# A graph attention kernel on one core: the group loop written out instead of branched

## What is computed

```
alpha = (x @ wq) @ (x @ wk)^T;  alpha = relu(alpha) * (adj != 0);  softmax over axis 1
y     = layernorm(x + alpha @ (x @ weight))
q, k, v = y @ Wq + bq, y @ Wk + bk, y @ Wv + bv      (16 heads of 32)
s     = q k^T / sqrt(32), -inf where adj == 0;  softmax
out   = layernorm(y + (softmax(s) @ v) @ Wo + bo)
```

## Time and profile before

| | |
|---|---|
| time, median of 3 runs (lowest to highest) | 3041.84 us (3039.97 to 3041.94) |
| span of the profiled execution | 3040.6 us |
| time around that span | 1.2 us to the median |
| mean granted TensorE clock | 0.991 |
| PE busy | 2912.7 us, 96% |
| DVE busy | 2383.2 us, 78% |
| ACT busy | 2023.8 us, 67% |
| POOL busy | 583.4 us, 19% |
| DMA queue of the kernel's data | 22.6% of 16 engines |

### The profile page before, as it was taken

How to read it: one execution, slowest core, us unless ns; L and a number is a source line. 1 busy time by engine, 2 the same in 40 slices (tenths; PEclk the granted TensorE clock), 3 DMA queues, 4 the chain that set the end, 5 groups by cost and what they waited for, 6 DMA issues and landing times. The chain is left out here.

```text
span 3040.6 us, 73236 instructions
## 1 busy us (share of the span) xinstructions
PE 2912.7 (96%) x24264; PEld 1775.8 (58%) x24264; DVE 2383.2 (78%) x4627; ACT 2023.8 (67%) x6414; POOL 583.4 (19%) x1289
## 2 busy tenths in 40 slices
PE   7899999999999999999999999999999999999996
PEld 4565665555665556555556655556655566555564
DVE  4577887777877778877788877778877778777786
ACT  3576776666666666666667666766766666666675
POOL 1111122121122111121121221111221211211120
PEclk9999999999999999999999999999999999999997
DMA  3222112222122222122221122221122221222211
GB/s 118 60 71 74 45 49 73 52 73 73 37 57 59 66 73 62 35 70 52 73 73 49 48 70 52 73 73 43 51 67 58 73 73 32 62 56 70 73 41 33
DMA packets 96225, 185.44 MB, mean 61 GB/s; under 512 B 18608, under 2 KB 34992, under 8 KB 96048
## 3 DMA queue, kind: packets, MB, share of 16 engines
q1 hardware_dynamic: 96048, 183.84, 22.6%
HBM read 49.55 MB, written 33.55 MB: 27 GB/s over the span
## 5 line engine op out<-in xcount | busy, mean ns | idle before, releaser
L647 ACT ACTIVATE e<-sm,nmax 128x128 f32<-128x128 f32 x2048 | 791.2, 391 | 27.6 <-DVE nmax L776 25.5
L598 ACT ACTIVATE qk<-front,bqk 128x512 f16<-128x512 f32 x256 | 175.9, 687 | 379.6 <-PE front L429 379.6
L825 POOL TENSOR_TENSOR ln<-ln 128x1 f32<-128x1 f32 x256 | 49.4, 193 | 1895.3 <-DVE ln L804 1490.8
L647 ACT ACTIVATION_READ_ACCUMULATOR e<-sm,nmax 128x1 f32 x2048 | 390.9, 191 | 0.0
L664 DVE SCALAR_TENSOR_TENSOR pT<-pt_bank,pT 128x512 f16<-128x512 f32 x512 | 349.4, 682 | 37.9 <-ACT pT L653 37.4
L653 ACT ACTIVATE pT<-pt_bank 128x512 f16<-128x512 f32 x512 | 302.6, 591 | 103.2 <-PE pt_bank L543 101.5
L776 DVE TENSOR_REDUCE nmax<-sm 128x4 f32<-128x512 f32 x512 | 351.3, 686 | 17.7
L429 PE MATMUL fin_bank<-W_O,oT 128*128 128x512 f16 x1536 | 356.2, 382 | 1.4 <-DVE oT L664 1.4
L429 PE MATMUL front<-W,bT 128*128 128x512 f16 x1536 | 347.2, 379 | 7.1 <-DVE bT L664 7.0
L429 PE MATMUL front<-W_V,yT 128*128 128x512 f16 x1536 | 354.0, 380 | 0.0
L429 PE MATMUL front<-xT,W_A 128*128 128x512 f16 x1536 | 353.7, 380 | 0.3 <-DVE xT L664 0.3
(11 more groups left out here) (111 smaller groups left out, 4489.5 us busy)
## 6 DMA issues: line engine op xcount, KB each, us to landing
q_st<-qk SPq DMA_DIRECT2D x384, 128.0 KB, 2.4
k_st<-qk SPq DMA_DIRECT2D x384, 128.0 KB, 2.4
x_sb<-in_x SPq DMA_DIRECT2D x128, 256.0 KB, 3.2
out_x<-z_sb SPq DMA_DIRECT2D x128, 256.0 KB, 2.1
adj_i<-in_adj SPq DMA_DIRECT2D x32, 256.0 KB, 4.0
y_sb<-in_L_gnn_wq SPq DMA_DIRECT2D x1, 1024.0 KB, 5.5
yb<-in_L_gnn_wk SPq DMA_DIRECT2D x1, 1024.0 KB, 8.3
x_p<-in_L_gnn_weight SPq DMA_DIRECT2D x1, 1024.0 KB, 10.3
```

What stands on the lines that cost most here:

```text
L598: i = act.activation(dst, src, ACT.Identity, bias=bias, scale=scale)
L647: act.activation(e1[:, k % 2, h, :], sm[:, k % SM_BUFS, h, :], ACT.Exp, bias=nmax[:, k % SM_BUFS, h:h + 1], accum_out=esum[:, n % 2, head: ...
L825: pool.tensor_tensor(ln[:, 8:9], ln[:, 7:8], ln[:, 8:9], ALU.add).then_inc(moments, 1)
```

## The change

On all five engines the loop statement is replaced by a Python loop that emits the same steps 30 times, with the group as a constant. The steps, their order, the buffers, the semaphores and the values that are waited for stay the same. The register arithmetic, the register operands of waits and DMA addresses, and all backward branches are no longer in the program; the program gets longer by 29 bodies on each engine.

```diff
@@ -302,9 +302,9 @@
             for p in (0, 1):
                 for what, k in order(0, p):
                     step(what, k, (None, p - age(what, k)))
-            with eng.Fori(2, groups) as i:
+            for g in range(2, groups):
                 for what, k in order(0, 2):
-                    step(what, k, (i, -age(what, k)))
+                    step(what, k, (None, g - age(what, k)))
             for what, k, n in drain_order():
                 step(what, k, (None, groups - n))
@@ -410,10 +410,10 @@
             load((None, 1))
             run(late, (None, 0), (0,))
             run(early, (None, 1), (0, 1))
-            with sp.Fori(2, groups) as i:
-                load((i, 0))
-                run(late, (i, -1), (0, 1))
-                run(early, (i, 0))
+            for g in range(2, groups):
+                load((None, g))
+                run(late, (None, g - 1), (0, 1))
+                run(early, (None, g))
             run(late, (None, groups - 1), (0, 1))
```

## The result

The changed kernel takes 2969.49 us (median of 4 runs, 2968.59 to 2969.97), the kernel before 3041.35 us (4 runs, 3039.97 to 3041.94). The ratio is 0.9765, with a 95% interval of 0.9751 to 0.9779: 2.35% less. The predicted time was 2968.5 us.

A forecast was written before the change was run, and what follows sets the result against it. PE and what it waits for were taken to bound the kernel, with ACT's branch ending last at each turn. Branch 69.1 plus registers 4.2, 73.3 us off the 3040.6 us span, plus 1.2, gave 2968.5 us; range 2963 to 2985.

The forecast's parts named there:

- The branch, 69.1 us: At each loop turn ACT restarts late at `xT 0` and PE waits; removing the branches gives 69.1 us.
- The mark to mark measurement: PE's first transpose to first `v` matmul: 5.28 us at a turn, 2.91 us entering pass 2, so 2.37 us a turn.
- PE's idle time of 58.2 us: PE's transposes of L468 waiting for DVE's `xT`, 30 cases; if only this came back, 2983.6 us.
- DVE's branch: At the turn DVE starts 0.04 us after ACT's first half ends; any branch time of its own lay under ACT's.
- The clock in pass 3, 1.7 us within the 66.7: Half clock for 3.5 us behind the first branch stall, expected gone without the stall: some 1.7 us.
- the 66.7: Branch gain in us over the 28 passes from pass 3's first transposes to pass 31's, at 89.80 us each.
- Registers, 4.2 us: PE's register waits at `alpha 0` and `g 0` cost 0.07 us each, over 30 passes 4.2 us; other register work nothing.
- The stacks: SP's last `k_st` DMA lands before PE's `S 0` reads it; with shorter turns 1.5 us are left, still holding.
- Code to fetch: PE's written-out body streams in, some 6 packets a pass, 174 more; taken as costing nothing.
- The sum: Branch 69.1 plus registers 4.2 gives 73.3 us off the 3040.6 us span: 2967.3 us.
- From the span to the time: The median stands 1.2 us above the profiled span, so 2967.3 us of span becomes 2968.5 us.

The follow-up runs named there:

- act_free: Kernel before with only ACT's loop written out, PE, DVE, POOL and SP still looped: 2970.11 us, ratio 0.9766.
- act_loop: Changed kernel with only ACT looped over passes 2 to 31, the other four engines written out: 3041.44 us, ratio 1.0001 to before.
- act_pairs: Changed kernel with only ACT in a loop, over pairs of groups, 14 backward branches: 3003.28 us, ratio 0.9875.
- dve_loop: Changed kernel with only DVE looped, the other four engines written out: 2969.01 us, ratio 0.9762.
- dve_held: Changed kernel with only DVE looped, its last step pT 14 given a second, always fulfilled wait to hold its stream back: 2968.50 us, ratio 0.9763.
- pe_loop: Changed kernel with only PE looped, the other four engines written out: 2969.80 us, ratio 0.9766.

## Why the prediction was right

The mechanism was right, and so was the sum over the passes. That the total agrees within 0.3 us of span is in part luck, as said under the sum.

- **The branch, 69.1 us.** The passes went from 92.18 to 89.66 us; 0.14 of that was put down to registers, so 2.38 us a pass were the branch's, as forecast from the pass of before that has no branch stall in it (the first in the loop, 89.80 us). `act_free`, `act_loop` and `act_pairs` (3003.28 for 3003) show that it is ACT's branch, and by the branch. The mark to mark measurement was needed: PE's idle time of 58.2 us alone would have given 2983.6 us.
- **DVE's branch.** "Any branch time of its own lay under ACT's" left open how much there was. It had nearly none to hide: `dve_loop` and `dve_held`.
- **The clock in pass 3, 1.7 us within the 66.7.** Gone, as forecast; pass 3 took 93.7 us where the passes behind it took 92.2, so it was worth 1.5. The cause isn't as firm as it was put, as such stretches come at one turn of 29 in the kernel before and at six with the same stall in `act_loop`.
- **Registers, 4.2 us.** 0.07 us at `alpha 0` is confirmed by the rows, and 0.15 us a pass, 4.1 us in all, by `pe_loop`. Its time doesn't show them, since its tail was as much shorter.
- **The stacks.** They held, with less room than forecast, and two errors stand behind the figure. The 2.4 us to landing were added to the end of the issue instead of its start, which made the room too small: 1.5 us instead of the 1.6 to 1.9 that the passes have with PE looped. And the cost of PE's code was mis-sized: "I take nothing" is true of PE and false of SP, whose DMA issue it delays by up to 1.5 us, so that in the tightest pass 0.3 us were left. The row was there in the trace of before, ahead of the turn into pass 2: pass 1 is written out, one packet of q8 lies in this stretch, and the issue took 8.39 us where those of the loop's passes took 7.5. The prediction looked at PE's idle time only.

```profile
195.73 8.39 SPq L388 DMA_DIRECT2D k_st<-qk  x12
```

- **Code to fetch.** 176 packets more, 174 forecast, and no stall of PE.
- **The sum.** 73.3 us forecast, 73.0 us by span (3040.6 to 2967.6). In the 29 passes from the first transposes of pass 2 to those of pass 31 it is 70.7 us (2670.92 to 2600.25), and the forecast's share of them is 66.7 us and 29 x 0.14 = 4.1 us, 70.8. This part is no luck. Behind the first transposes of pass 31 the forecast had 2.5 us and 0.8 came, since a stretch at the lower clock follows there in the changed kernel and not in the one before (12 matmuls of `v` take 4.31 us from 2892.13, against 2.75 us). And 1.5 us came ahead of pass 2, where the two programs are the same and nothing was forecast. This start differs between kernels for no reason that was found: the first transpose of pass 2 comes at 197.6 to 201.2 us in the kernels with the stacks as they were. That the two nearly cancel is luck.
- **From the span to the time.** The forecast added 1.2 us, the median of before less one span. In the changed kernel the run that gave the span took 1.8 us more than it. That and the 0.3 us of the sum make 2969.49 out of 2968.5.

## What to carry to other kernels

Count the idle rows that nothing releases and look whether their number is that of the backward branches; then find one turn in the trace without a branch, such as a loop's entry, and measure from mark to mark there. It is enough to treat the one engine whose body is too long: write it out, name the branch ahead, or turn its loop where that engine waits for another anyway; here all three gave the same within 0.15%. Where the program is written out, check the transfers with the least room, for a packet of code among them can hold up their issue.

## What the runs showed of the hardware

- A backward branch is cheap or dear by the length of the body. ACT and DVE paid about 0.5 to 0.75 us with 96 to 224 operations and 2.7 to 3.9 us with 288 and more; PE up to 1.6 us with 600 matmuls, and 4.6 to 5.2 us with 900 and more. On the cheap side PE fetched no code at its turns, on the dear side some 9 packets of 16 KB at each.
- A hint that names the branch didn't move the fetches but ended them: 13 packets on q14, where 158 had gone, 143 of them in passes 3 to 31.
- With a 16 KB packet of TensorE's code among them, the issue of SP's 12 DMAs took 7.60 to 9.03 us (14 passes), without one 7.49 to 7.89 us (16 passes).
- The time to landing on the profile's page runs from the start of the issue: 1099.22 us and 2.5 us, with the reader at 1102.13.
- Under a repeated stall of PE of 2.0 to 2.2 us at one place, the granted clock fell to its lower level at one turn of 29 in one kernel and at six of 29 in another with the same stall.
